# An attention loop with t and P in fp32, stacked token halves for t and the gates, and u of one step beside the scores of the next

## What is computed

```python
zn = (z - mu) * rsqrt(var + EPS) * ln_w + ln_b              # z = _gn(x), per token over 32 channels
q = (zn @ Wq).reshape(n, l, l, H, C); k = (zn @ Wk)...; v = (zn @ Wv)...      # H = 8, C = 16
g = sigmoid(zn @ Wg + bg).reshape(n, l, l, H, C)
att = einsum('iabhc,jabhc->ijabh', q, k) * (1.0 / sqrt(C))  # attention over the 16 n, at each (a, b)
att = softmax(att, axis=1)
o = einsum('ijabh,jabhc->iabhc', att, v) * g
x = x + o.reshape(n, l, l, H * C) @ Wo + bo
```

## Time and profile before

| | |
|---|---|
| median of 3 runs | 345.29 us |
| profiled execution | 347.44 us, span 345.5 us |
| before t of step 0 starts | 36.4 us |
| passes of the attention loop, with their tail | 36.4 to 263.4 us |
| one pass in the middle | 25.2 or 25.3 us |
| second block | 263.4 to 345.5 us |
| busy: VectorE, TensorE, ScalarE, GpSimd | 258.1, 249.6, 217.3, 195.8 us |

### The profile page before, as it was taken

One profiled execution on the slowest core, in us unless ns is written; L12 is line 12 of the kernel. 1 busy time (PEld: TensorE's weight loads), 2 busy tenths in 40 slices (PEclk: granted clock), 3 DMA queues, 4 the chain that ended last, 5 costly groups with the idle time before them and its releaser, 6 DMA issues.

```text
span 345.5 us, 7455 instructions
## 1 busy us (share of the span) xinstructions
PE 249.6 (72%) x2982; PEld 151.5 (44%) x2982; DVE 258.1 (75%) x466; ACT 217.3 (63%) x392; POOL 195.8 (57%) x169
## 2 busy tenths in 40 slices
PE   0056965599779779679679669769864599998724
PEld 0046342377347346346346347346531145554223
DVE  4985789766797898898898895899796764431972
ACT  4635787389569669669579669468341447567512
POOL 6890564659885896886877843434840862000620
PEclk9995799658998999999999998998997599999856
DMA  7100122013031031031031022100000014667207
GB/s 248 31 0 30 33 63 63 0 39 86 0 93 32 2 92 35 1 93 32 5 88 34 30 64 55 40 0 3 2 2 0 1 30 93 169 183 199 62 0 243
DMA packets 34893, 19.66 MB, mean 57 GB/s; under 512 B 21228, under 2 KB 31788, under 8 KB 34860
## 3 DMA queue, kind: packets, MB, share of 16 engines
q1 hardware_dynamic: 34860, 19.20, 20.7%
HBM read 8.71 MB, written 6.29 MB: 43 GB/s over the span
## 4 chain that ended last, share of the span: by engine, by line
DVE 41%; PE 36%; ACT 14%; issue 7%; DMA 1%; POOL 1%; DVEq 0%; ACTq 0%
PE PS L1126 31%; DVE t_sb L876 6%; DVE nmax L892 5%; DVE S_sb L896 4%; DVE og L869 4%; DVE gn_part L964 3%; DVE sums L820 3%; ACT u_sb L593 2%; ACT PP L623 2%; DVE Z L1113 2%; DVE Z L1117 2%; PE PS L1390 2%; ACT t_sb L607 2%; PE PS L1195 1%; DVE st L830 1%
## 5 line engine op out<-in xcount | busy, mean ns | idle before, releaser
L1126 PE MATMUL PS<-znT,A_bd 128*128 128x512 f16 x192 | 46.9, 387 | 11.8 <-DVE t_sb L876 10.5
L427 POOL TENSOR_TENSOR S_sb<-S_sb,rden 128x512 f32<-128x512 f32 x32 | 35.5, 1133 | 27.7 <-DVE rden L838 27.7
L876 DVE TENSOR_TENSOR t_sb<-PS,t_sb 128x512 f16<-128x512 f32 x64 | 41.1, 683 | 8.6 <-ACT t_sb L607 8.6
L607 ACT CAST t_sb<-PS 128x512 f16<-128x512 f32 x64 | 36.6, 611 | 15.0 <-PE PS L1126 13.5
L613 ACT ACTIVATE S_sb<-S_sb 128x512 f32<-128x512 f32 x32 | 20.2, 631 | 31.8 <-DVE S_sb L896 31.8
L1126 PE MATMUL PS<-zbd,t_sb 128*128 128x64 f16 x768 | 28.9, 199 | 13.6 <-DVE t_sb L876 12.8
L433 POOL TENSOR_TENSOR PP<-S_sb,PP 128x512 f16<-128x512 f32 x28 | 31.8, 1158 | 12.0 <-ACT PP L601 12.0
L1126 PEld LDWEIGHTS PS<-zbd,t_sb 128*128 128x128 f16 x768 | 26.0, 102 | 25.1 <-DVE t_sb L876 16.7
L1126 PE MATMUL PS<-PP,Z 128*128 128x128 f16 x512 | 34.6, 236 | 0.2 <-DVE PP L850 0.2
L593 ACT COPY u_sb<-PS 128x512 f32<-128x512 f32 x64 | 33.7, 626 | 1.6 <-PE PS L1126 1.4
L1126 PEld LDWEIGHTS PS<-znT,A_bd 128*128 128x128 f16 x192 | 16.9, 99 | 40.6 <-DVE t_sb L876 23.9
(11 more groups left out here) (198 smaller groups left out, 529.5 us busy)
## 6 DMA issues: line engine op xcount, KB each, us to landing
Z<-zn_dram SPq DMA_DIRECT2D x64, 64.0 KB, 2.8
x_tok<-in_x SPq DMA_DIRECT2D x4, 512.0 KB, 5.6
zn_dram<-zn_tok SPq DMA_DIRECT2D x8, 256.0 KB, 2.0
zbd<-znT SPq DMA_DIRECT2D x32, 64.0 KB, 2.0
k_dram<-og SPq DMA_DIRECT2D x4, 512.0 KB, 3.6
th<-k_dram SPq DMA_DIRECT2D x16, 128.0 KB, 2.7
out_x<-u_sb SPq DMA_DIRECT2D x4, 512.0 KB, 3.3
PP<-u_sb SPq DMA_DIRECT2D x8, 128.0 KB, 2.4
```

Of the source, the lines that this page charges most:

```text
L427: nc.gpsimd.tensor_tensor(P, P, bcast(rden[:, 32 * k:32 * k + 32], 2, N), ALU.mult).then_inc(p_nrm, 1)
L607: nc.scalar.copy(t_sb[:, HI, :, h], bank_tg(h)[:, :].rearrange("p (q i) -> p q i", i=N)).then_inc(t_hi, 1)
L876: nc.vector.tensor_tensor(t_sb[:, LO, :, h], bank_tg(h)[:, :].rearrange("p (q i) -> p q i", i=N), t_sb[:, HI, :, h], ALU.subtract).then_in ...
L1126: return nc.tensor.matmul(o, l, r, start=start, stop=stop)
```

## The change

t, P and the attention's z are kept in fp32 (`t_sb`, `S_sb`, `zbd`, `Zmem`): the scores are one fp32 matmul per position, u is one fp32 matmul of 64 rows per position, and P is transposed as 16 blocks of two positions. For t and the gates, the token halves are stacked in 96 rows of `zst` (high, low, high), against `A_st` with (high, high, low) of the weights, so that one f16 matmul does the work of three; t is now four matmuls per head, each for one group e of 32 output rows. To fill `zst`, ScalarE writes the f16 high half and the fp32 z out of PSUM, VectorE the low half, and SP issues twelve DMAs of 32 rows by 512 columns. t then needs one ScalarE copy per head. P needs no split. S is double-buffered, and PT and u of step j-1 stand in pass j between the scores of step j, so the loop ends one pass earlier for u. u is copied by ScalarE (5 of 8) and VectorE (3 of 8). The statistics are summed up by GpSimd in `acc`, the layer norm's centring goes to GpSimd, and the second block's weights are prepared by VectorE in pass 0.

The core of the diff:

```diff
-        t_sb = sb("t_sb", [128, 2, QS, H, N], f16)
-        S_sb = sb("S_sb", [128, QS, A2, N])
-        PP = sb("PP", [128, 2, QS, 128], f16)
-        P2 = PP[:, 0].rearrange("p q (k m) -> p q k m", k=2)
-        PT = PP[:, 1]
+        zTf = sb("zTf", [128, COLS])
+        zhl = sb("zhl", [128, 2, COLS], f16)
+        zbd = sb("zbd", [128, A2, COLS])
+        Zmem = sb("Zmem", [128, 8192])
+        Z = Zmem[:, 0:4096].rearrange("p (r m x) -> p r m x", r=2, m=QS // 2)
+        t_sb = sb("t_sb", [128, QS, H, N])
+        S_sb = sb("S_sb", [128, 2, QS, A2, N])
+        PP = sb("PP", [128, 4096])
+        zst = PP[:, 2048:4096].bitcast(f16).rearrange("p (k e x) -> p k e x", k=2, e=A2)
+        PT = PP[:, 0:2048].rearrange("p (m x) -> p m x", m=QS // 2)
...
+        def sp_feed(sp, j):
+
+            par, half = j % 2, j // 2
+            wait_z(sp, j)
+            for r in range(2):
+                sp.dma_start(zn_dram[j, r].rearrange("n f b e d -> (n f) (b e d)"),
+                             zc[r::2, par].rearrange("p b e d -> p (b e d)")).then_inc(zn_st[par], 16)
+            sp.wait_ge(zT_l, j + 1)
+            for p, k in enumerate((HI, LO, HI)):
+                for e in range(A2):
+                    sp.dma_start(zst[D * p:D * p + D, par, e], zhl[D * e:D * e + D, k]).then_inc(zs_ld[par], 16)
+            if j >= 1:
+                sp.wait_ge(s_mm, 4 * j)
             for e in range(A2):
                 rows = slice(D * e, D * e + D)
-                sp.dma_start(zbd[rows, e], znT[rows]).then_inc(zbd_ld, 16)
-            if not last:
-                sp_store(sp, j + 1, 1 - par)
-            else:
+                sp.dma_start(zbd[rows, e], zTf[rows]).then_inc(zbd_ld, 16)
+            if j >= 2:
                 sp.wait_ge(u_mm, 8 * (j - 1))
-            sp.wait_ge(zn_st[par], 16 * (half + 1))
-            for copy in range(2):
+            sp.wait_ge(zn_st[par], 32 * (half + 1))
+            for r in range(2):
                 for e in range(A2):
-                    r0 = 64 * copy + N * e
-                    sp.dma_start(Z[r0:r0 + N, par, :, :, e].rearrange("p f k d b -> p f k (d b)"),
-                                 zn_dram[:, :, bass.ds(j, 1), :, e].rearrange("n f s k m -> n (f s) k m")
+                    r0 = 64 * r + N * e
+                    sp.dma_start(Z[r0:r0 + N, par, :, D * e:D * e + D],
+                                 zn_dram[j, r, :, :, :, e].rearrange("n f b d -> n (f b) d")
                                  ).then_inc(Z_ld[par], 16)
...
+        def act_zT(act, j):
             act.wait_ge(zT_mm, j + 1)
-            src = bank_w[:, :].bitcast(f16).rearrange("p (k n f) -> p k f n", f=A4, n=N)
-            dst = znT[:, :, :].rearrange("p k c -> p (k c)").rearrange("p (k f n) -> p k f n", f=A4, n=N)
-            nc.scalar.copy(dst, src).then_inc(zT_ok, 1)
+            if j >= 1:
+                act.wait_ge(zs_ld[(j - 1) % 2], 192 * ((j - 1) // 2 + 1))
+            nc.scalar.copy(z_cols(zhl[:, HI]), zT_bank()).then_inc(zT_h, 1)
+            if j >= 1:
+                act.wait_ge(zbd_ld, 64 * j)
+            nc.scalar.copy(z_cols(zTf[:, :]), zT_bank()).then_inc(zT_f, 1)
...
+        def dve_zT_low(dve, j):
+            dve.wait_ge(zT_f, j + 1)
+            nc.vector.tensor_tensor(z_cols(zhl[:, LO]), zT_bank(), z_cols(zhl[:, HI]), ALU.subtract).then_inc(zT_l, 1)
...
+            if j == 0:
+                dve_weights2(dve)
+                dve_biases2(dve)
...
-        def pe_znT(pe, j, par):
-            wait_zn(pe, j)
-            if j >= 3:
-                pe.wait_ge(x1_ok, j - 2)
-            zt = bank_w[:, :].bitcast(f16)
-            tok = zn_tok[:, par].rearrange("p k e d b -> p k (e d) b")
-            for k in (HI, LO):
-                for b in range(SB):
-                    at = 128 * (SB * k + b)
-                    last = nc.tensor.transpose(zt[:, at:at + 128], tok[:, k, :, b], ident16[:, :])
+        def pe_zT(pe, j):
+            wait_z(pe, j)
+            if j >= 1:
+                pe.wait_ge(g_th, HP * j)
+            for b in range(SB):
+                last = nc.tensor.transpose(bank_w[:, 128 * b:128 * b + 128],
+                                           zc[:, j % 2, b].rearrange("p e d -> p (e d)"), ident[:, :])
             last.then_inc(zT_mm, 1)
 
-        def pe_t(pe, j, hs=range(H)):
-            if hs[0] == 0:
-                pe.wait_ge(zT_ok, j + 1)
+        def pe_t(pe, j, hs):
             for h in hs:
+                if h == 0:
+                    pe.wait_ge(zs_ld[j % 2], 192 * (j // 2 + 1))
+                if h < 3 and j >= 1:
+                    pe.wait_ge(g_th, HP * (j - 1) + 3)
+                if h in (1, 2) and j >= 2:
+                    pe.wait_ge(u_ok, 5 * (j - 1))
                 if h >= 3:
-                    pe.wait_ge(t_lo, H * j + h - 2)
-                elif j >= 1:
-                    pe.wait_ge(g_th, HP * (j - 1) + h + 2)
-                split_mm(bank_tg(h)[:, :], [A_bd[:, k, h].rearrange("p e d -> p (e d)") for k in (HI, LO)],
-                         [znT[:, k] for k in (HI, LO)]).then_inc(t_mm, 1)
+                    pe.wait_ge(t_ok, H * j + h - 2)
+                for e in range(A2):
+                    last = mm(bank_tg(h)[D * e:D * e + D, :], A_st[0:96, h], zst[0:96, j % 2, e])
+                last.then_inc(t_mm, 1)
...
-                    last = split_mm(bank_s(k)[:, 64 * (q % 8):64 * (q % 8) + 64],
-                                    [t_sb[:, p, q].rearrange("p h i -> p (h i)") for p in (HI, LO)],
-                                    [zbd[:, :, p, N * q:N * q + N] for p in (HI, LO)])
+                    last = mm(bank_s(k)[:, 64 * (q % 8):64 * (q % 8) + 64],
+                              t_sb[:, q].rearrange("p h i -> p (h i)"), zbd[:, :, N * q:N * q + N])
...
+        def pe_u(pe, m, g):
+            if g == 0:
+                pe.wait_ge(Z_ld[m % 2], 128 * (m // 2 + 1))
+                pe.wait_ge(pt_ok, 4 * m + 4)
+            if g >= 2:
+                pe.wait_ge(u_ok, 5 * m + g - 1)
+                pe.wait_ge(u_od, 3 * m + g - 1)
+            for i in range(4):
+                for r in range(2):
+                    rows = slice(64 * r, 64 * r + 64)
+                    last = mm(bank_u(g, r)[:, 128 * i:128 * i + 128], Z[rows, m % 2, 4 * i + g], PT[rows, 4 * g + i])
+                    if i == 3:
+                        last.then_inc(u_mm, 1)
...
+        def pe_period(pe, j):
+
+            s, m = j - 2, j - 1
+            A, B = j < NS, 1 <= j <= NS
+            if A:
+                pe_t(pe, j, (0, 1, 2))
+            if s >= 0:
+                pe_o(pe, s)
+            if A:
+                pe_t(pe, j, range(3, H))
+            if s >= 0:
+                pe_out(pe, s)
+            if A:
                 pe_scores(pe, j, (0, 1))
+            if B:
+                if j == 1:
+                    pe.wait_ge(wprep_a, 8)
+                pe_PT(pe, m, (0, 1))
+            if A:
                 if j == 0:
                     pe.wait_ge(wprep, WP1)
+                    pe.wait_ge(wprep_a, 5)
                 pe_gate(pe, j, (0, 1))
+            if B:
+                pe_PT(pe, m, (2, 3))
+            if A:
                 pe_scores(pe, j, (2,))
+            if B:
+                pe_u(pe, m, 0)
+            if A:
                 pe_scores(pe, j, (3,))
+                pe_gate(pe, j, (2,))
+            if B:
+                pe_u(pe, m, 1)
             if A:
+                pe_gate(pe, j, (3,))
+            if B:
+                pe_u(pe, m, 2)
+            if j + 1 < NS:
+                pe_zT(pe, j + 1)
+            if B:
+                pe_u(pe, m, 3)
```

More of the change, by code:

```diff
@@ L605, in t_high @@
                 for h in hs:
                     act.wait_ge(t_mm, H * j + h + 1)
-                    nc.scalar.copy(t_sb[:, HI, :, h], bank_tg(h)[:, :].rearrange("p (q i) -> p q i", i=N)).then_inc(t_hi, 1)
-            def exps(ks):
-                for k in ks:
-                    act.wait_ge(s_sub, 4 * j + k + 1)
-                    v = S_sb[:, 8 * k:8 * k + 8].rearrange("p q a n -> p (q a n)")
-                    nc.scalar.activation(v, v, ACT.Exp).then_inc(s_exp, 1)
-            def gates(ks):
-                for k in ks:
-                    act.wait_ge(g_mm, HP * j + k + 1)
-                    nc.scalar.activation(th[:, par, k], bank_tg(H + k)[:, :], ACT.Tanh, bias=bg_h[:, :],
-                                         scale=0.5).then_inc(g_th, 1)
@@ new lines, in gate, with u_copy @@
+            def gate(k):
+                act.wait_ge(g_mm, HP * j + k + 1)
+                nc.scalar.activation(th[:, j % 2, k], bank_g(k)[:, :], ACT.Tanh, bias=bg_h[:, :],
+                                     scale=0.5).then_inc(g_th, 1)
+            def PT_copy(k):
+                act.wait_ge(pt_mm, 4 * m + k + 1)
+                nc.scalar.copy(PT[:, 4 * k:4 * k + 4].rearrange("p m x -> p (m x)"), bank_b(k)[:, :]).then_inc(pt_ok, 1)
+            def u_copy(g, r):
+                act.wait_ge(u_mm, 8 * m + 2 * g + r + 1)
```

(63 more changed lines are left out.)

569 lines of the change are left out of this document (229 added, 340 removed).

## The result

The changed kernel takes 414.52 us (median of 4 runs, 414.13 to 416.06) against 345.15 us for the kernel before (345.0 to 345.47, 4 runs on the same chip): a ratio of 1.2017, 95% interval 1.1985 to 1.2048. It is 20% slower. The forecast was 435 us in 398 to 480, slower with 0.95.

The account below looks back on a forecast made before the run. Bound before: two copying engines, VectorE and ScalarE, with DMAs hidden. First passes to 113.8, five of 37.4 to 300.8, scores at 310.5, tail 43 to 353.5, second block 82.1: span 435.6, forecast 435 us, range 398 to 480.

Parts of the forecast that it names:

- mechanism: Between z and the next t: twelve DMA issues in place of four, and t waits for them with little left beside them.
- The middle pass: Attention loop, start of t to start of the next t: 35.0 us at full clock, 37.4 with the low clock, against 25.3.
- sign: In the profile after, passes of 35 to 40 us would show the forecast right; a pass under 30 us, wrong.
- The way from z to t: Twelve DMAs, 0.63 us apart with 0.5 more for the first, then 2.0 to land: 9.4 us before t starts.
- T: Start of t of step j, from which the forecast counts a pass up to the start of t of step j+1.
- The low half: VectorE's low half of the transposed z: ends 25.5 us after the start of t, at full clock.
- The clock: TensorE at the lower level, 1.2 GHz, when t starts, rising within t and o: 2.4 us a pass.
- rival of one latency for all: Twelve DMAs issued together share a latency and land after some 2.6 us, no gap: 375 us, chance 0.03.
- fp32 scores: Score matmuls on TensorE, decided by their weight load: 0.215 us each, 32 taking 6.9 us at full clock, 14.5 at half.
- Weights in pass 0: VectorE prepares the second block's weights from 62.0, estimated 13 us, to 75; scores of pass 1 start at 83.7, not 79.
- The tail: Emptying the pipe, from the start of the last scores to the loop's end: about 43 us, to 353.5; before it was 41.2.
- Not slower: Rival: way from z back to t hidden altogether, ScalarE binding at 23.5 us a pass: 339 us, chance 0.04.

Follow-up runs that it names:

- number 1: Changed kernel with ScalarE issuing six of the twelve DMAs for steps 1 to 7 and SP the other six: 392.88 us.
- numbers 2: Changed kernel with `zst` filled for two steps only, so steps 2 to 7 use stale tokens and t doesn't wait for transfers: 367.29 us.
- 6: Changed kernel reordered, nothing left out: layer norm, z's transposes and copies and the twelve DMAs earlier in the pass, gates off z's bank: 364.22 us.
- Number 4: Changed kernel with 72 unused fp16 matmuls on TensorE in each gap between the last u and the next t: 412.85 us.
- numbers 5: Changed kernel with each fp32 score matmul replaced by three fp16 ones on constants, scores not the reference's: 380.41 us.
- 7: Changed kernel with z's work and DMAs earlier in the pass, and three fp16 matmuls on constants for each fp32 score matmul: 337.14 us.
- early-z order: Changed kernel's work reordered so that z and its twelve DMAs come earlier, beside the second half of a pass: 364.22 us without further edits.
- number 8: Kernel of the early-z order with the second block's weights and biases prepared in the pass behind the last step: 367.14 us.
- number 3: Changed kernel with the second block's weights and biases prepared in passes 3 and 4 instead of at the end of pass 0: 414.66 us.

## Why the prediction was right, and where it was off

The mechanism is shown: number 1 halves the issues and the gap shortens by 3.5 us a pass, and numbers 2 and 6 take away the transfers or move them, and the gap is gone. The number was 20 us too high, the sum of errors of both signs. By the steps of the sum:

| | forecast | measured |
|---|---|---|
| t of step 0 | 42.4 | 41.8 |
| t of step 1 | 71.5 | 75.3 |
| t of step 2 | 113.8 | 111.2 |
| t of step 7 | 300.8 | 282.9 |
| its scores | 310.5 | 291.2 |
| end of the loop | 353.5 | 330.0 |
| end | 435.6 | 412.8 |

- *The middle pass, 37.4 against 34.3*, just under the 35 to 40 given as a sign. Three terms make the 3.1. The way from z to t was 9.4 and is 8.84: the issues start 0.63 apart as taken, but the 0.5 allowed ahead of the first isn't there (0.02), and the landing is 1.83 for 2.0. The scores were to start at T + 9.7, 7.3 and 2.4 for the clock, and start at T + 8.5: 1.2. Number 4's warm pass parts the two: 6.6 without the low clock, and 1.9 for the clock. The low half was to end at T + 27.9 and ends at T + 25.4, so with that 1.2 another 1.3 is gone; 0.9 of it lies in the eight pieces of ScalarE from 192.99 to 197.23, which follow each other 0.53 apart and not 0.61 or more.
- *The clock.* Direction and place were right: 0.50 at T, back within o. Its size was 1.9 a pass where I took 2.4: o loses 1.1 of the 2.35 given, as the rise comes in its middle, and t ahead of it loses 0.6 (1.47 us for twelve matmuls, 0.83 when warm). The Trainium skill, "TensorE: Matmul & The Clock Gate", Part 1, has the throttled level as the default and activity as what releases it. The passes of this trace agree: 0.50 in the idle gap, 1.00 again in t and o. Number 6 doesn't: TensorE was busy 86% and more, and had half clock for 60 us. There the measurement decides.
- *Issues.* The rival of one latency for all is dead: SP's line 295 takes 557 to 607 ns for one issue, 96 times, and ScalarE's queue about 0.6 us. The Trainium skill, "DMA: Bandwidth & Descriptors", "Anatomy of one DMA", gives about 50 ns of sequencer dispatch, for GpSimd's path; SP's rows differ from that by a factor of ten.
- *fp32 scores.* 0.215 us each was the estimate, 0.237 is the reading (3.79 over 16 matmuls of two records). (The 0.43 for a record of 512 columns isn't in the earlier trace rows, where ten in 3.6 us are 0.36 each; the sum doesn't use it.) u, taken as 1.3 a group, takes 1.16, and t's column groups do run together. The prediction had the scores in its pass and didn't ask what they cost against fp16: numbers 5 and 7 show 27 to 34 us for the matmuls, the second cause, which I would have called the lesser one by far. At half clock 16 of them take 7.09 us, and in pass 0 all 32 are slow; with 2 us for the clock there, I had its length too short by 4.4 (29.1 against 33.5).
- *Weights in pass 0.* The step failed. I put 13 us and a delay of the scores to T + 12.2; they took 6.9, the gap covered them, and the scores started at T + 5.7. That and the too short pass 0 all but cancel at t of step 2. In the early-z order, where the cover is gone, pass 1 is 11.7 us shorter without the same work (number 8); part of that is the clock, which came back at 78.9 there and at 100.9 in number 6.
- *The tail.* Forecast 43, measured 38.8, from the last scores (291.2) to 330.0. Three terms were too long: the last u of step 6 ends after 15.4 us (17.7), P and u of step 7 take 7.4 (9.5), and what follows the last o takes 5.5 (7.4). The two stretches with o were too short by 1 us each, as a copy of u (1.1) stands ahead of either.
- *Not slower* needed the way from z to t hidden altogether and gave 339. Number 6 hides it, and takes 364: the low clock in passes 0, 1 and 4 to 6 and the fp32 scores stand in its place. Of the 24.0 us of its pass 2 ScalarE is busy 15.0 and TensorE 21.3, so ScalarE isn't the fuller of the two.

## What to carry to other kernels

A transfer is cheap only where nothing waits for it: before its consumer is changed, ask who needs it first, how many issues stand one behind the other on the queue, and what work is left to lie beside them. If the issues can't be fewer, spread them over two queues, or move the producer up until they lie beside other work; here that was worth 22 us, and 50 with the low clock that the gap had brought. And fewer matmuls aren't less time when each is fp32. Price them by the record (two per fp32 matmul) and not by the columns, at the low clock too: at 1.2 GHz, 16 records with 32 columns took 3.63 us in the kernel before, 0.227 each, and 32 with 64 columns take 7.09 here, 0.222 each.

## What the hardware showed beside this

- A small VectorE copy can stand still behind GpSimd: the 32 by 32 copy of 0.17 us took 4.69 and ended at 263.43, 0.03 us after GpSimd's memset (263.40); the 128 by 128 cast of 0.23 took 3.39 and ended 0.07 after the second (274.24). In number 3, where the biases are prepared beside GpSimd's layer norm, the same cast took 0.96 and 1.17 us and ended within 0.1 us of a GpSimd instruction's end (174.64 and 174.56, 176.92 and 176.83); in the changed kernel, with GpSimd idle, it took 0.23. The Trainium skill, "SBUF — State Buffer", "SBUF: two separate sides", tells of a port pair that VectorE's 2-port modes and GpSimd lock against each other for a whole instruction; these rows fit that. That they are short with GpSimd idle and long beside it is shown; that the lock is the reason is argued.
- The clock fell in passes in which TensorE was busy 24.75 of 27.5 us (number 6), while the kernel before held 1.00 with 20.1 busy of 25.3; in other passes it fell there too (0.94 over 92.9 to 119.6, with 21.6 of 26.7 busy). Why is open.
- Executions of the early-z kernels spread by 2 to 4% (357.6 to 367.4 in number 6), those of the changed kernel by 0.5%. That the low clock falls at other places in each, as no gap has a fixed place there, is a guess: each kernel has one trace.
